# Causal attention in pieces of 64 tokens on eight TensorE tiles instead of 128 tokens on four

## The reference, cut to what matters

```python
q = jax.nn.silu(x @ Wq); k = jax.nn.silu(x @ Wk); v = x @ Wv     # 16 heads of 16 channels
q = _lrpe(q, theta); k = _lrpe(k, theta)                          # 16 -> 32 channels per head
mask = jnp.tril(jnp.ones((n, n)))
energy = jnp.einsum('bhnd,bhmd->bhnm', q, k) * mask
out = jnp.einsum('bhnm,bhmd->bhnd', energy, v)
...
h = alpha * h + bt        # causal_ema, one step per token, four averages of the gated input
...
x = x + attention(cond(x)); x = x + ffn(cond2(x))
```

## Time and profile before

| | |
|---|---|
| median of 3 runs | 664.17 us (664.09 to 664.36) |
| span of the profiled execution | 663.8 us; its own time is not listed, only the span |
| TensorE busy | 612.2 us, 92% of the span, 6824 matmul records |
| VectorE busy | 538.8 us, 81% |
| ScalarE, GpSimd busy | 285.8 us, 43%; 295.7 us, 45% |
| mean granted TensorE clock | 0.979 of 2.4 GHz |
| bytes moved | 52.84 MB, 80 GB/s |

### The profile page before, as it was taken

How to read it: one execution, slowest core, us unless ns; L and a number is a source line. 1 busy time by engine, 2 the same in 40 slices (tenths; PEclk the granted TensorE clock), 3 DMA queues, 4 the chain that set the end, 5 groups by cost and what they waited for, 6 DMA issues and landing times.

```text
span 663.8 us, 17064 instructions
## 1 busy us (share of the span) xinstructions
PE 612.2 (92%) x6824; PEld 439.4 (66%) x6854; DVE 538.8 (81%) x1092; ACT 285.8 (43%) x597; POOL 295.7 (45%) x320
## 2 busy tenths in 40 slices
PE   5796989999999999999999999999999999998763
PEld 3565667767777677777777676777766766666341
DVE  6797777788896969787897969787897989988764
ACT  2563533444444444444444444445435352553311
POOL 0157755253453635162543635162565603746132
PEclk9897999999999999999999999999999999999886
DMA  8400703032313232133413232233421340061512
GB/s 317 171 2 2 216 17 98 2 88 74 107 34 72 67 88 82 48 99 81 114 33 74 73 84 79 50 96 82 109 54 37 93 114 17 17 154 25 113 32 71
DMA packets 81919, 52.84 MB, mean 80 GB/s; under 512 B 59058, under 2 KB 75698, under 8 KB 81330
## 3 DMA queue, kind: packets, MB, share of 16 engines
q1 hardware_dynamic: 81554, 51.20, 28.7%
q10 hardware_dynamic: 288, 0.57, 0.3%
HBM read 34.83 MB, written 8.53 MB: 65 GB/s over the span
## 4 chain that ended last, share of the span: by engine, by line
PE 70%; DVE 16%; POOL 5%; issue 4%; DMA 3%; ACT 1%; SPq 0%; POOLq 0%; DVEq 0%
PE ps L483 64%; PE ps L486 7%; DVE B L897 3%; DVE EB L897 2%; DVE CT L1023 2%; DVE FT L906 1%; DVE ZN L903 1%; POOL RS L1178 1%; DMA HQ<-HP 1%; DVE HP L897 1%; POOL RS L1157 1%; DMA B<-g_rows 1%; POOL HP L1204 1%; DVE WS L906 1%; DMA g_rows<-G 1%
## 5 line engine op out<-in xcount | busy, mean ns | idle before, releaser
L1178 POOL TENSOR_SCALAR RS<-MV,EPS 128x1 f32<-128x1 f32 x32 | 14.4, 449 | 209.1 <-DVE MV L1007 209.1
L897 DVE TENSOR_TENSOR B<-B,BLGS 128x1024 f32<-128x1024 f32 x64 | 92.6, 1489 | 3.3 <-DMA B<-g_rows 3.2
L483 PE MATMUL ps<-WQ,YT 128*128 128x512 f32 (+1 forms) x256 | 91.7, 500 | 1.1 <-ACT YT L741 0.9
L897 DVE TENSOR_TENSOR EB<-ps,C 128x512 f32<-128x512 f32 x128 | 79.2, 681 | 7.7 <-PE ps L483 7.4
L483 PEld LDWEIGHTS ps<-WQ,YT 128*128 128x128 f32 x256 | 47.1, 192 | 38.8 <-issue 28.0
L741 ACT ACTIVATE FH<-ps,AM 128x512 f32<-128x512 f32 x64 | 43.5, 687 | 43.8 <-PE ps L483 41.4
L1204 POOL TENSOR_SCALAR HP<-HP,FT 128x1024 f32<-128x1024 f32 x32 | 39.0, 1218 | 50.0 <-DVE FT L900 49.9
L1157 POOL TENSOR_TENSOR KP<-TH,CS 128x512 f32<-128x512 f32 x32 | 43.3, 1356 | 36.7 <-ACT TH L741 19.3
L483 PE MATMUL ps<-FW,ZQ 128*128 128x512 bf16 x226 | 54.5, 380 | 4.0 <-ACT ZQ L741 1.5
L741 ACT ACT_TABLE_LOAD x41 | 52.6, 1283 | 2.3 <-PEq L1298 1.6
L897 DVE TENSOR_TENSOR HP<-FH,ps 128x512 f32<-128x512 f32 x64 | 42.2, 682 | 10.4 <-ACT FH L741 10.2
(11 more groups left out here) (136 smaller groups left out, 1355.2 us busy)
## 6 DMA issues: line engine op xcount, KB each, us to landing
B<-g_rows SPq DMA_DIRECT2D x32, 512.0 KB, 4.2
XT<-xT SPq DMA_DIRECT2D x16, 256.0 KB, 4.3
X<-x SPq DMA_DIRECT2D x32, 128.0 KB, 3.6
g_rows<-G SPq DMA_DIRECT2D x32, 128.0 KB
out<-X SPq DMA_DIRECT2D x32, 128.0 KB, 2.0
CW<-condW SPq DMA_DIRECT2D x8, 257.0 KB, 3.0
HP<-ffnw SPq DMA_DIRECT2D x2, 1024.0 KB, 5.4
W<-wpack SPq DMA_DIRECT2D x1, 1841.0 KB, 11.1
```

Source lines behind the costliest of these rows:

```text
L483: return e0.matmul(o, l, r, start=start, stop=stop, skip_group_check=True)
L897: return e0.tensor_tensor(o, x, y, op)
L1178: e0.tensor_scalar(RS[:, s, 0:1], MV[:, s, 1:2], EPS[:, 0:1], None, ALU.add).then_inc(g["rs0"], 1)
```

## The change

The attention works on units of 256 tokens, cut into pieces of 64 tokens: `h` is the half of a chunk, `k` the chunk of the unit, and `j` counts the eight pieces of a sequence.

- `energies(u)`: per unit 64 matmuls, 32 rows deep, 64 keys by 64 queries, on the eight tiles of 32x64. The products between the two halves of a chunk are no longer made.
- `gains(u)` (new job `s`): k^T v of every piece by itself, 64 matmuls per unit (48 in a sequence's last unit, which leaves out its last chunk's second half), 64 rows deep and 64 columns wide, on the eight tiles of 64x32. `V` is twice as wide, with each head's 16 values in 64 columns of zeros, so the result needs no masking.
- `ss(u)` (new job on VectorE): four (three in a sequence's last unit) operations of 128x256 build the running states in `SS`: a copy for a sequence's first piece, else an add of the gain in PSUM and the state before.
- `carried(u)` (new job `a`): states times `QT`, 8 matmuls per piece except a sequence's first, 64 columns, on 128x32 tiles. `outs(u)` (job `o`): 64 matmuls of 64 columns, 64 rows deep, on the eight tiles of 64x32, added to what `a` left in the two banks `oa` and `ob`.
- `em(u)`: four `TENSOR_TENSOR` of 128x512 per unit, as many as there were per chunk.
- `ema`: the product of `PX` and `UB` is cut into four matmuls on the 128x32 tiles.
- The states' own bank is gone and the ring has 8 banks. `TT` and `TP` hold one unit instead of two, and some constants are loaded into `TT` before it is in use.
- All ten tables of jobs are new; `PERIODS` is `range(2, 13)` as before.

```diff
-RING = 7
+RING = 8
-        V = sb("V", [P, 2, 512])
+        V = sb("V", [P, 2, 1024])
-        SS = sb("SS", [P, 2, CH])
+        SS = sb("SS", [P, 4, CH])
-        TT = sb("TT", [P, 2, NT])
+        TT = sb("TT", [P, 2, CH])
-        TP = sb("TP", [P, 2, NT])
+        TP = sb("TP", [P, 2, CH])
-            "o": lambda n: (a["ot"], n + 1), "wo": lambda n: (v["og"], n + 1), "xtr": lambda n: (a["x1t"], n + 1),
+            "sa": lambda n: (v["ss"], states(n) + 3), "sb": lambda n: (v["ss"], states(n) + 4 - 2 * (n % 2)),
+            "oa": lambda n: (a["ot"], 2 * n + 1), "ob": lambda n: (a["ot"], 2 * n + 2), "wo": lambda n: (v["og"], n + 1), "xtr": lambda n: (a["x1t"], n + 1),
...
-        def states(c):
-            return 3 * (c // 4) + min(c % 4 + 1, 3)
+        def states(u):
+            return 7 * (u // 2) + 4 * (u % 2)
...
-                for i in range(4):
-                    for n in range(4):
-                        m = mm(bank(f"e{n}", c)[:, i * P:(i + 1) * P], KT[32 * n:32 * n + 32, s, i * P:(i + 1) * P],
-                               QT[32 * n:32 * n + 32, s, i * P:(i + 1) * P])
+                for k in range(2):
+                    for i in range(4):
+                        for n in range(4):
+                            for h in range(2):
+                                tok = slice(i * P + 64 * h, i * P + 64 * h + 64)
+                                m = mm(bank(f"e{n}", u)[64 * h:64 * h + 64, (4 * k + i) * 64:(4 * k + i + 1) * 64],
+                                       KT[32 * n:32 * n + 32, k, tok], QT[32 * n:32 * n + 32, k, tok])
...
+            def gains(u):
+                e.wait_ge(g["rk"], 2 * u + 2)
+                e.wait_ge(a["vg"], 2 * u + 2)
+                e.wait_ge(*emptied("sa", u))
+                e.wait_ge(*emptied("sb", u))
+                for k in range(2):
                     for i in range(4):
-                        for r in range(0, P, 32):
-                            m = mm(SB[r:r + 32, i * 64:(i + 1) * 64], KP[:, s, i * P + r:i * P + r + 32], vgroup(s, i),
-                                   j == 0 and i == 0, i == 3)
+                        for n in range(4):
+                            for h in range(1 if u % 2 and k else 2):
+                                m = mm(bank("sb" if h else "sa", u)[32 * n:32 * n + 32, k * 256 + i * 64:k * 256 + (i + 1) * 64],
+                                       KP[64 * h:64 * h + 64, k, i * P + 32 * n:i * P + 32 * n + 32],
+                                       V[64 * h:64 * h + 64, k, i * 256 + n * 64:i * 256 + (n + 1) * 64])
+                m.then_inc(t["s"], 1)
+
+            def carried(u):
+                e.wait_ge(v["ss"], states(u) + 3)
...
+                for h in range(2):
+                    first = True
+                    for k in range(2):
+                        j = 4 * (u % 2) + 2 * k + h
+                        if j:
+                            for i in range(4):
+                                for r in range(2):
+                                    q = 2 * (i % 2) + r
+                                    m = mm(bank("ob" if h else "oa", u)[32 * q:32 * q + 32, (2 * k + i // 2) * 64:(2 * k + i // 2 + 1) * 64],
+                                           SS[:, j % 4, i * 64 + 32 * r:i * 64 + 32 * r + 32],
+                                           QT[:, k, i * P + 64 * h:i * P + 64 * h + 64], first and i < 2, False)
...
+            def outs(u):
+                e.wait_ge(v["em"], 4 * (u + 1))
...
+                                    m = mm(bank("ob" if h else "oa", u)[32 * q:32 * q + 32, (2 * k + half) * 64:(2 * k + half + 1) * 64],
+                                           V[64 * h:64 * h + 64, k, i * 256 + n * 64 + n // 2 * 32:i * 256 + n * 64 + n // 2 * 32 + 32],
+                                           EB[64 * h:64 * h + 64, n, 4 * k + i, :], False, w == 1)
...
-                mm(bk[:, 0:256], PX[:, j * P:(j + 1) * P], UB[:, c // 4 % 2, :], False, True).then_inc(t["ema"], 1)
+                for r in range(0, P, 32):
+                    m = mm(bk[r:r + 32, 0:256], PX[:, j * P + r:j * P + r + 32], UB[:, c // 4 % 2, :], False, True)
+                m.then_inc(t["ema"], 1)
...
-                    tt(EB[:, i, :, :], bank(f"e{i}", c)[:, :].rearrange("p (g n) -> p g n", g=4),
-                       mask.unsqueeze(1).to_broadcast([P, 4, P]), ALU.mult).then_inc(v["em"], 1)
+                    tt(EB[:, n, :, :], bank(f"e{n}", u)[:, :].rearrange("p (g n) -> p g n", g=8),
+                       mask.unsqueeze(1).to_broadcast([P, 8, 64]), ALU.mult).then_inc(v["em"], 1)
...
+            def ss(u):
+                e.wait_ge(t["s"], u + 1)
+                e.wait_ge(t["a"], u)
+                for k in range(3 if u % 2 else 4):
+                    j = 4 * (u % 2) + k
+                    gain = bank("sb" if k % 2 else "sa", u)[:, k // 2 * 256:k // 2 * 256 + 256]
+                    if j:
+                        e.wait_ge(v["ss"], states(u) + k)
+                        tt(SS[:, (j + 1) % 4, :], gain, SS[:, j % 4, :], ALU.add).then_inc(v["ss"], 1)
+                    else:
+                        e0.tensor_copy(SS[:, 1, :], gain).then_inc(v["ss"], 1)
```

One entry of the tables on each side, the start of TensorE's period:

```diff
 PE_PERIOD = (
-    ("ema", 2, -4), ("h1", 1, -1), ("soma", 1, -1), ("gate", 1, 0), ("o", 2, 0), ("ema", 2, -3), ("ktr", 2, 1), ("wg", 2, -2),
+    ("proj", 2, 7), ("ktr", 2, 6), ("xtr", 2, 4), ("gu", 2, -1), ("xtr", 2, 5), ("ema", 2, 2), ("h1", 1, 2), ("ema", 2, 3),
```

More of the change, by code:

```diff
@@ L28 @@
 _off = 0
-for _n, _w in (("ident", 128), ("mask", 128), ("diff", 32), ("low", 32), ("sub", 4), ("ncol", 4), ("tail", 1), ("pexp", 512)):
+for _n, _w in (("ident", 128), ("mask", 64), ("pexp", 512), ("diff", 32), ("low", 32), ("sub", 4), ("ncol", 4), ("tail", 1)):
     CP[_n] = (_off, _off + _w)
@@ L32 @@
 CPN = _off
+CPS = CP["diff"][0]
 PE_HEAD = (
[L38 to L41, removed]
@@ new lines @@
+    ("ztr", 0), ("ktr", 7), ("qtr", 7), ("ztr", 1), ("wg", 5), ("gu", 0), ("cond", 4), ("s", 3), ("mod", 2), ("e", 3), ("proj", 8),
+    ("a", 3), ("o", 3), ("ktr", 8), ("ttr", 1), ("wo", 6), ("wo", 7), ("temp", 1), ("proj", 9), ("wout", 2), ("qtr", 8), ("xtr", 6),
+    ("wout", 3), ("xtr", 7), ("cond", 5), ("u", 2), ("low", 4), ("h1", 3), ("ema", 4), ("soma", 3), ("ztr", 2), ("ktr", 9),
+    ("wg", 6), ("gu", 1), ("wg", 7), ("ema", 5), ("mod", 3), ("gate", 4), ("qtr", 9), ("ttr", 2), ("gu", 2), ("dn", 0), ("e", 4),
@@ L50 @@
+    ("a", 1, 3), ("low", 1, 4), ("o", 1, 3), ("u", 1, 2), ("qtr", 2, 8), ("wo", 2, 6), ("wo", 2, 7), ("wout", 2, 2), ("wout", 2, 3),
+    ("cond", 1, 5), ("dn", 2, -1),
 )
 PE_TAIL = (
[L52 to L54 removed]
@@ L55 @@
[L55 to L58, removed]
@@ L287, in build @@
         banks = [ctx.enter_context(nc.psum_tensor(f"ps{i}", [P, 512], f32)) for i in range(8)]
-        SB = banks[7]
-        d = sems("dma", "ids cpk thb wq wpk bgb ubl xt0 xt1 cw" + "".join(f" ff{i}" for i in range(3))
+        d = sems("dma", "ids cpk cps thb wq wpk bgb ubl xt0 xt1 cw" + "".join(f" ff{i}" for i in range(3))
                  + "".join(f" x{j}" for j in range(NJ)) + "".join(f" st{i}" for i in range(6)) + " uw blg mw0 mw1 mr0 mr1 gw0 gw1 gr0 gr1 hq0 hq1")
-        t = sems("pe", "wsum cond proj lo gate qtr ktr e smm o wo xtr h1 mod wg soma u ema ttr temp wout ztr gu dn")
+        t = sems("pe", "wsum cond proj lo gate qtr ktr e s a o wo xtr h1 mod wg soma u ema ttr temp wout ztr gu dn")
         a = sems("act", "lo tg sin p2 sp tab ex yt th vg qT kT ot x1t h1 mt wgt sm tk tt tp zq fh")
@@ L728, in wsum @@
                 mm(bank("wsum", n)[:, 0:1], ONES[:, :].to_broadcast([P, P]), WS[:, n:n + 1]).then_inc(t["wsum"], 1)
-            does = {"cond": cond, "proj": proj, "low": low, "gate": gate, "qtr": qtr, "ktr": ktr, "e": energies, "o": outs, "wo": wo, "xtr": xtr,
+            does = {"cond": cond, "proj": proj, "low": low, "gate": gate, "qtr": qtr, "ktr": ktr, "e": energies, "s": gains, "a": carried, "o": outs, "wo": wo, "xtr": xtr,
                     "h1": h1, "soma": soma, "mod": mod, "wg": wg, "u": ends, "ema": ema, "ttr": ttr, "temp": temp,
```

178 lines of the change are left out of this document (86 added, 92 removed), and 112 rows, old and new, of tables (ACT_HEAD, ACT_PERIOD, ACT_TAIL, DVE_HEAD).

## The result

The changed kernel takes **726.4 us** (median of 4 runs, 719.3 to 729.1) against 664.3 us for the one before on the same chip: 1.091 times as long, 95% interval 1.087 to 1.095. The prediction was 639 us in a range of 626 to 661, faster. It was wrong in sign, and by 87 us.

What follows compares the result with a forecast made beforehand. TensorE's own work was taken to bound eleven of sixteen units; 21.3 us saved in attention and 6.2 in the averages made 27.5 less work, 24.9 of it counting: 663.8 to 638.9 us of span, 639 us, range 626 to 661.

Steps and rivals of the forecast that it cites:

- What bounds the kernel now: In eleven of sixteen units nothing but TensorE's own work fills the 37.15 us period; head and tail wait for others.
- Does it count in full?: Saved TensorE work counts fully in eleven units (18.9 us), at 0.7 in the other five (6.0 us): 24.9 us.
- the sum: TensorE's attention work 4.10 us per unit, 65.6 instead of 86.9 us; with the averages' 6.2 us, 27.5 us less work.
- What a record of 64 columns costs: On TensorE, a round of eight 64-column records on eight tiles takes 0.059 us, with 0.118 as the other end.
- rival 2: On TensorE, handing over records partly holds back rounds of eight, at 0.070 to 0.096 us: 653 us; chance 0.14.
- ema: TensorE's averages take 1.42 us per chunk instead of 1.61, as PX times UB is cut in four: 6.2 us saved.
- The new waits: Between gains and outputs TensorE has 7.2 us of work, VectorE needs 5.1 for states and masks: 2.1 us left.
- my bound of 36.5: The prediction counts as wrong if TensorE's period, forecast at 35.4 us, stays above 36.5 us.
- Rival 3: New order waits: VectorE reaches the states 3 us late, TensorE waits 0.9 us per unit: 653 us; chance 0.08.
- What happens elsewhere: VectorE saves 39.6 of 79.2 us of masks, state operations rise 10.0 to 23.2; net 26.4 us less, still covered.
- The rule weighed: Skill's 60 cycles of overhead per matmul: 424 records at 25 ns, attention 10.6 us per unit, kernel about 743 us.
- rival 1: On TensorE, only four tiles work at once or records come no faster, 0.118 us a round: 680 us; chance 0.12.

Runs made afterwards that it cites:

- r4_wide: Changed kernel with energies, gains and outputs as half as many matmuls of 128 columns instead of 64, output not the attention's: 654.4 us, 0.985 of before.
- r2_burst: Kernel before with five runs of 192 added, unused matmuls at TensorE's start, on four kinds of small tiles and the whole array: 786.3 us, measured once.
- r1_px_only: Kernel before with only the product of PX and UB cut into four matmuls on 128x32 tiles: 660.95 us, 0.9943 of before.
- r7_blocks: Kernel before with added groups of 64 matmuls, 0 to 4 of them long, then 768 bf16 matmuls, ahead of TensorE's jobs: 804.1 us, measured once.

## Why the prediction was wrong, step by step

- **"What bounds the kernel now"** held for the kernel before: TensorE's work fills its period.
- **"Does it count in full?" is the step that failed.** It carried this over to the changed kernel, where TensorE was to be busy throughout, and left its idle time at 54.2 us. The supply of instructions had no term in the sum, though the change raises the instructions from 13678 to 21260. It measured 38.9 us more of "issue", and some 17 us of slower matmuls at the half clock behind the stops: about 56 of the 87.8 us by which the forecast's span was off. The queue of instructions stood in the page with 0.6% of the DMA engines' time, which says nothing of how fast one block follows another.
- **"What a record of 64 columns costs" was mis-sized too**, by some 17 us in all, which alone would have left the time inside the range. I took 0.059 us for a round of eight. Rounds in the changed kernel, with nothing stopping them: energies (1.57 - 0.23) / 16 = 0.084 us, outputs (1.42 - 0.11) / 16 = 0.082, gains (1.50 - 0.11) / 16 = 0.087. That lies inside rival 2's 0.070 to 0.096 us: a record comes every 10 to 12 ns where the sum needed 7.4. r4_wide shows that the geometry was right: with records of 128 columns energies take 1.13 us where the sum had 1.17, outputs 1.08 for 1.05, and gains 1.03 in the units with 48 records. The sum had 0.82 for these (12 rounds) and counted wrongly: the last chunk's second half is left out, so its first half runs on four tiles only, and 96 records of 64 columns are 8 rounds of eight and 8 of four, 16 in all. The carried part, which no width was changed of, takes 0.92 us for 64 records (308.65 to 309.57). Halving the length of a record on eight tiles was assumed to halve its time, and the row with 15 ns per record of 8 columns had already hinted that it doesn't. I set it aside as the end of a stage; r2_burst has 14.8 ns for 8 columns in long runs, at the half clock. What in the handing over of records sets the 10 to 12 ns, no run here separates.
- **Against the forecast's span of 638.9 us** the profiled 726.7 stand 87.8 higher, in two parts. r4_wide has a span of 651.0: 12.1 us belong to the order and the rest of the sum. Its TensorE is busy for 587.0 us, 25.2 less than before where I said 27.5, and idle for 64.0 where the forecast leaves 54.2. The other 75.7 us lie between r4_wide and the changed kernel: 38.9 us of "issue" (44.4 less 5.5); about 1.1 us per unit, 17 us, for handing over records (0.44 in the energies, 0.34 in the outputs, 0.2 in the gains of 96 records and some 0.4 in those of 128); and 20 us that remain. Most of these lie in the matmuls right behind a stop: `TT,W` is busy for 43.0 us in the changed kernel (first row below) and 31.9 in r4_wide (second), and `WQ,YT` of 512 columns for 67.0 and 60.7 us in the same view. These 17 us go with the half clock. How the other 3 divide I did not separate.

```profile
L465 PE MATMUL ps<-TT,W 128*128 128x256 f32 x128 | 43.0, 495 | 0.7 <-ACT TT L745 0.7
```

```profile
L465 PE MATMUL ps<-TT,W 128*128 128x256 f32 x128 | 31.9, 390 | 1.7 <-issue 1.0 <-ACT TT L744 0.7
```

- **"ema"** was right for the work (0.87 and 0.55 forecast, 0.86 and 0.43 found where the same shape follows), and in the period it counted in full in r1_px_only (0.38 us of 0.39). Of the 6.2 us for the whole about 3.5 came; the rest was lost in the head and the tail.
- **"The new waits"**: VectorE is in time for the states and the mask; `QT,SS` and `EB,V` start without a wait in the rows above, and neither `SS` nor `EB` stands in the view of its waits. What the order does cost is 0.57 us per period for `CT` (335.11 us in r4_wide, and the same in the changed kernel), which I had not looked at. The period of r4_wide is 36.5 us (`TT,W` starts at 309.52 in one unit and at 346.00 in the next), not the 35.4 forecast but just at my bound of 36.5; the changed kernel's is 42.6 (301.14 to 343.73). Rival 3 in its own form did not come.
- **"What happens elsewhere"**: the mask took 39.7 us as forecast. VectorE in all has 530, not 512, and the forecast had no term for it. The same operations became slower in the new order: the scans of `CT` went from 28.6 to 40.1 us (mean 0.94 to 1.29 us), `B` times `BLGS` from 92.6 to 100.4. Why, no run here shows. It stayed covered but for the wait for `CT`.
- **The rule weighed** came nearer to the time than the sum, but not by its mechanism. Where nothing stops it, attention takes about 5.2 us per unit in the changed kernel (1.57, 1.23 or 1.50, up to 0.92, and 1.42), half of what 424 records at 25 ns would make and a little less than before (86.9 / 16 = 5.4). The Trainium skill, TensorEngine Tiling (Array Packing), Instruction Overhead, warns against small free sizes, and with 64 columns on eight tiles that warning holds; its 60 cycles for each matmul do not, if a record counts as one: they come at 10 to 12 ns here, and the 224 records in bf16 of r7_blocks, one to a matmul, at 2.28 / 224 = 10 ns. The prediction counted by records. Counted by f32 matmuls of two records, these stages take 22 to 25 ns for each, near the 25 ns of the rule.
- **The chances**: rival 1 had 0.12 and rival 2 0.14, and neither contained the cause. The range had no room for a cost that no row of before shows.

## What to carry to other kernels

Count TensorE's instructions as well as its columns: a matmul of f32 is four. Wherever a whole block of 256 is less than about 3.6 us of work, expect a stop (where the blocks begin is not seen in the code, and one dense stage of 256 instructions can pass without one, as the outputs at 309.90 us do). Put a long matmul between two dense stages (18 us came back from moving two jobs) or make each matmul longer. And read a rate from the shortest records in the trace, not from the longest that still look full.
